# Attention on one core: queries and values computed token by token, mixing matrices in blocks of 64, two batch halves attended together, and the fourth normalisation placed among the attention's instructions

## The reference

```
x = x + conv_gate(_ln_c(x))        # gates; one needs the 0.85 quantile of |x| of each image
t = t + moe(_ln_t(t))              # router, 2 of 8 experts
x = x + attention(_ln_c(x))        # the part that is changed
t = t + ffn(_ln_t(t))              # 8 experts, weights from the mean token

# attention, for each image: q is 8 heads x 16, k and v are 16 wide and shared by all heads
q, k, v = Wq x + bq, Wk x + bk, Wv x + bv
k = softmax(k, over the 256 tokens);  q = softmax(q, over the 16 of a head)
context = k v^T (16 x 16);  out = q context;  y = Wo out + bo
```

## Time and profile before

| | us |
|---|---|
| runs | 245.97, 247.32, 249.61 |
| profiled execution | 246.73 |
| its span in the trace | 244.9 |

### The profile page before, as it was taken

The page is one execution under the profiler, slowest core; times in us unless marked ns, Lnnn a source line. Parts: engine busy times, 40 slices in busy tenths (PEclk is TensorE's granted clock), DMA queues, the critical chain, the costliest instruction groups (busy, mean ns, idle before and its releaser), DMA issues.

```text
span 244.9 us, 3059 instructions
## 1 busy us (share of the span) xinstructions
PE 191.9 (78%) x1077; PEld 78.2 (32%) x1077; DVE 158.1 (65%) x296; ACT 115.8 (47%) x193; POOL 73.9 (30%) x81
## 2 busy tenths in 40 slices
PE   7971478388899689988786788643999999999971
PEld 4310123133261222222222567311346345333220
DVE  1564889674749766687547875998361436647772
ACT  2498677134678765500066924441062695465200
POOL 7710876003699000000350053665340071000000
PEclk9997555559997999999999959997696799999998
DMA  6993100000000000000000000000000000001011
GB/s 185 353 209 76 27 1 0 0 1 0 3 1 3 0 1 3 0 0 0 0 0 3 0 0 3 1 0 1 0 0 3 0 0 0 24 22 46 0 44 43
DMA packets 4291, 6.44 MB, mean 26 GB/s; under 512 B 626, under 2 KB 3954, under 8 KB 4130
## 3 DMA queue, kind: packets, MB, share of 16 engines
q1 hardware_dynamic: 3700, 5.73, 8.6%
q10 hardware_dynamic: 576, 0.52, 0.7%
HBM read 3.99 MB, written 1.05 MB: 21 GB/s over the span
## 4 chain that ended last, share of the span: by engine, by line
PE 47%; DVE 23%; ACT 12%; issue 7%; POOL 6%; DMA 3%; SPq 1%; DVEq 0%
PE ps L742 5%; PE ps L607 4%; PE ps L335 4%; PE ps L753 4%; PE ps L582 4%; PE ps L766 4%; PE ps L329 3%; POOL hidden_of_all_tokens L339 3%; PE ps L555 3%; POOL gated_x L1510 2%; DVE hidden_of_all_tokens L353 2%; PE ps L594 2%; PE ps L570 2%; DVE hidden_of_all_tokens L1288 2%; PE ps L702 2%
## 5 line engine op out<-in xcount | busy, mean ns | idle before, releaser
L339 POOL TENSOR_TENSOR hidden_of_all_tokens<-hidden_of_all_tokens 128x512 f32<-128x512 f32 x16 | 18.5, 1166 | 64.8 <-DVE hidden_of_all_tokens L353 64.8
L1003 ACT ACTIVATE hidden_of_all_tokens<-ps,bn_shift,bn_scale 128x512 f32<-128x512 f32 x32 | 23.2, 776 | 19.9 <-PE ps L742 19.9
L1412 DVE SCALAR_TENSOR_TENSOR gated_x<-ps,bn_shift_negated,hidden_of_all_tokens 128x512 f32<-128x512 f32 x32 | 22.5, 746 | 14.8 <-PE ps L756 13.6
L345 ACT ACTIVATE hidden_of_all_tokens<-ps,weights 128x512 f32<-128x512 f32 x16 | 10.9, 683 | 42.5 <-PE ps L335 40.1
L1288 DVE TENSOR_TENSOR hidden_of_all_tokens<-hidden_of_all_tokens,ps 128x512 f32<-128x512 f32 x32 | 20.5, 683 | 8.7 <-PE ps L594 8.5
L934 ACT ACTIVATE hidden_of_all_tokens<-ps,weights 128x512 f32<-128x512 f32 x32 | 19.9, 685 | 9.5 <-PE ps L582 9.2
L353 DVE COPY hidden_of_all_tokens<-ps 128x512 f32<-128x512 f32 x16 | 11.1, 692 | 19.1 <-PE ps L329 14.0
L742 PE MATMUL ps<-x_normed,weights 64*64 64x512 f32 x128 | 23.2, 656 | 0.2 <-ACT hidden_of_all_tokens L1003 0.2
L335 PE MATMUL ps<-hidden_of_all_tokens,weights 128*128 128x512 f32 x32 | 17.3, 628 | 5.3 <-POOL hidden_of_all_tokens L339 5.1
L582 PE MATMUL ps<-x_normed,weights 64*64 64x512 f32 x128 | 18.4, 667 | 2.1 <-ACT hidden_of_all_tokens L934 2.0
L766 PE MATMUL ps<-gated_x,weights 64*64 64x512 f32 x32 | 16.5, 595 | 2.0 <-DVE x_resid L1420 1.4
(11 more groups left out here) (252 smaller groups left out, 408.0 us busy)
## 6 DMA issues: line engine op xcount, KB each, us to landing
weights<-in_weights SPq DMA_DIRECT2D x1, 2087.5 KB, 12.8
hidden_of_all_tokens<-hidden_of_all_tokens SPq DMA_DIRECT2D x8, 128.0 KB, 4.5
out_x<-x_resid SPq DMA_DIRECT2D x8, 128.0 KB, 2.4
x_resid<-in_x ACTq DMA_DIRECT2D x4, 128.0 KB, 3.2
x_resid<-in_x SPq DMA_DIRECT2D x4, 128.0 KB, 3.6
weights<-in_weights SPq DMA_DIRECT2D x1, 419.0 KB, 6.4
taps_shifted<-taps_padded SPq DMA_DIRECT2D x9, 18.1 KB
weights<-in_weights SPq DMA_DIRECT2D x1, 130.0 KB, 2.4
```

Source lines behind the costliest of these rows:

```text
L339: pool.tensor_tensor(SQ[:, cols(q)], XC[:, cols(q)], XC[:, cols(q)], ALU.mult).then_inc(sq_ready, 1)
L1003: act.activation(h1_tile(t), tile_of(t, Z1_BANK), ACT.Relu, bias=bn_c[:, p:p + 1], scale=bn_a[:, p:p + 1]).then_inc(h1_ready, 1)
L1412: dve.scalar_tensor_tensor(HW[:, t % PAIRS].rearrange("p (b n) -> p b n", n=N), tile_of(t, Z2_BANK).rearrange("p (b n) -> p b n", n=N), ne ...
```

## The change

Queries: T is now the stationary operand in blocks of 64 channels x 128 tokens, `wq` the moving one, so that queries come out with tokens on partitions. The bias is added by a bfloat16 matmul (a stack of three parts, `BQ`, against ones). DVE's two 32x32 turns per step are gone. ACT copies the queries to QB, the softmax is as before, four transposes on TensorE (`queries_back`) bring 128x512 queries back, and ACT stores them to QS (`queries_store`). Tile i is now half h of column group u, i = 2u + h, so `attend` and `attn_add` work on 512 columns and come four times. Keys are made in four row groups of 32 so that the softmax over tokens works on 128 partitions and two tiles; values are made with tokens on partitions by 16 matmuls. BD is made of 64x64 blocks. Normalisation 3 and `f_route` stand among the attention's instructions. SP issues 11 more transfers ahead of L415, with 32 or 128 pieces of 4 bytes each, and 6 more behind L430; POOL has 3 more memsets at its start and 5 small operations before the channel gating.

The cut below leaves out the lines that are removed (they stand above), the shapes of the new tiles, and functions whose body only changed in its tile.

```diff
...
-            return (0, 1, 4, 5)[q] if n == 2 else (0, 1, 5, 6)[q]
+            return ((0, 1, 5, 6), (0, 1, 5, 6), (0, 1, 4, 5), (2, 2, 0, 1))[n][q]
+        def query_bank(i):
+            return i % 2 + (4 if i // HALVES == 1 else 0)
+        def var_bank(n, q):
+            return 3 if n == 3 else 2 + q % 2
         def ln_pe_center(pe, n, q, x_wait):
...
+            a = AT["kv_bias"][0]
+            with nc.allow_non_contiguous_dma(reason="a column of biases"):
+                for j in range(4):
+                    sp.dma_start(kb4[32 * j:32 * j + 32, :], weights_dram[0:32, a:a + 1]).then_inc(kb_in, 16)
+                sp.dma_start(vb[:, :], weights_dram[32:64, a:a + 1]).then_inc(kb_in, 16)
             sp.wait_ge(rows_zeroed, 1)
+            a = AT["bq"][0]
+            with nc.allow_non_contiguous_dma(reason="a column of biases turned into rows"):
+                for h in range(HALVES):
+                    for k in range(PARTS):
+                        sp.dma_start(bq_rows[C * h + k:C * h + k + 1, :], weights_dram[:, a:a + 1].rearrange("p o -> o p")).then_inc(bq_in, 16)
             a, b = AT["sel"][0], AT["b2"][0]
             for h in range(HALVES):
                 for k in range(PARTS):
@@ -428,6 +456,11 @@
                     tap = 3 * dy + dx
                     off = LEAD + (dy - 1) * PITCH + dx - 1
                     sp.dma_start(SHIFTED[tap:18:TAPS, :], PADDED[tap:18:TAPS, off:off + FLAT]).then_inc(shifted_in, 16)
+            sp.wait_ge(bq_split, 4)
+            for h in range(HALVES):
+                for k in range(PARTS):
+                    at_row = slice(C * h + k, C * h + k + 1)
+                    sp.dma_start(BQ[at_row, :], bq_parts[at_row, k]).then_inc(bq_stacked, 16)
...
+            def queries(u):
+                if u == 1:
+                    pe.wait_ge(xc_copied, 3 * NQ)
+                if u >= 2:
+                    pe.wait_ge(q_copied, 4 * u - 6)
+                for h, rows in enumerate((LO, HI)):
+                    pe.matmul(PS[:, query_bank(2 * u + h)].rearrange("p (k c) -> p k c", c=P), ones16[rows, :], BQ[rows, :].unsqueeze(1).to_broadcast([C, 4, P]),
+                              start=True, stop=False, skip_group_check=True)
+                for k in range(4):
+                    for h, rows in enumerate((LO, HI)):
+                        last = pe.matmul(PS[:, query_bank(2 * u + h), cols(k, P)], T[rows, cols(4 * u + k, P)], w("wq", rows, cols(h, P)),
+                                         start=False, stop=True, skip_group_check=True)
+                last.then_inc(q_ready, 1)
+            def queries_back(i):
+                pe.wait_ge(qn_ready, i + 1)
+                pe.wait_ge(*((qs_ready, i - 1) if i >= 2 else (q_copied, 3 + i)))
+                for k in range(4):
+                    last = pe.transpose(PS[:, 4 + i % 2, cols(k, P)], QB[:, i % 4, cols(k, P)], w("ident"))
+                last.then_inc(qt_ready, 1)
+            def attend(u):
+                pe.wait_ge(qs_ready, 2 * u + 2)
+                if u >= 2:
+                    pe.wait_ge(x3_ready, u - 1)
+                for b in range(2):
+                    for h in range(HALVES):
+                        last = pe.matmul(PS[cols(h, C), 6 + u % 2, cols(b, N)], MB[:, h, 2 * u + b], QS[:, (2 * u + h) % 4, cols(b, N)], start=True, stop=True)
+                last.then_inc(a_ready, 1)
...
+                    queries(0)
...
+                for b in (2 * q, 2 * q + 1):
+                    j = b % 4
+                    last = pe.matmul(PS[32 * j:32 * j + 32, 6 + b // 4, 0:N], w("wkv", cols=slice(0, 32)), T[:, cols(b, N)], start=True, stop=True)
+                if q % 2:
+                    last.then_inc(k_ready, 1)
+                if q == 2:
+                    queries(1)
             pe.wait_ge(ln_taken, 3 * NQ)
+            for t in range(16):
+                last = pe.matmul(PS[:, 3, cols(t, 32)], T[:, cols(t, P)], w("wkv", cols=slice(32, 64)), start=True, stop=True)
+            last.then_inc(v_ready, 1)
...
+            def keys_turn(g):
+                pe.wait_ge(ek_ready, g + 1)
+                for jj in range(2):
+                    last = pe.transpose(PS[:, 6 + g, cols(jj, P)], EK[:, cols(2 * g + jj, P)], w("ident"))
+                last.then_inc(kt_ready, 1)
...
+            queries_back(0)
...
+            queries_back(1)
             queries(2)
-            queries(3)
-            for h in range(HALVES):
+            def mixes(h):
                 pe.wait_ge(bd_ready, h + 1)
                 for b in range(BH):
-                    last = pe.matmul(PS[:, 4 + h, cols(b, C)], BD[:, h * BH + b], w("wo"), start=True, stop=True)
+                    for rows in (LO, HI):
+                        last = pe.matmul(PS[rows, 6 + h, cols(b, C)], BD[rows, h * BH + b], w("wo", rows), start=True, stop=True)
...
+            mixes(0)
+            mixes(1)
+            queries_back(2)
+            queries_back(3)
+            queries(3)
+            pe.wait_ge(mb_out, HALVES)
+            attend(0)
+            queries_back(4)
+            center3(0)
+            queries_back(5)
+            attend(1)
+            ln_pe_var(pe, 3, 0)
+            queries_back(6)
+            center3(1)
+            queries_back(7)
+            attend(2)
+            ln_pe_var(pe, 3, 1)
+            attend(3)
+            pe.wait_ge(q_copied, BH)
+            center3(2)
+            f_route(0)
+            center3(3)
+            ln_pe_var(pe, 3, 2)
+            f_route(1)
+            ln_pe_var(pe, 3, 3)
+            f_route(2)
+            f_route(3).then_inc(fl_ready, 1)
...
+            def queries_out(i):
+                act.wait_ge(q_ready, i // HALVES + 1)
+                if i >= 4:
+                    act.wait_ge(qt_ready, i - 3)
+                act.activation(QB[:, i % 4], PS[:, query_bank(i)], ACT.Copy).then_inc(q_copied, 1)
...
+            def queries_store(i):
+                act.wait_ge(qt_ready, i + 1)
+                if i >= 4:
+                    act.wait_ge(a_ready, i // HALVES - 1)
+                act.activation(QS[:, i % 4], PS[:, 4 + i % 2], ACT.Copy).then_inc(qs_ready, 1)
...
             queries_out(0)
+            keys_exp(0)
             queries_out(1)
-            for g in range(2):
-                act.wait_ge(ekt_ready, g + 1)
-                act.activation(EKVT[:, cols(g)], PS[:, 4 + g], ACT.Copy).then_inc(ekt_out, 1)
+            keys_exp(1)
             queries_exp(0)
-            act.wait_ge(cx_ready, 1)
-            act.activation(CTX[:, :], PS[0:32, 2, 0:N], ACT.Copy).then_inc(cx_out, 1)
             queries_out(2)
+            act.wait_ge(v_ready, 1)
+            act.activation(V[:, :], PS[:, 3], ACT.Copy).then_inc(v_out, 1)
+            keys_out(0)
+            keys_out(1)
             queries_exp(1)
             queries_out(3)
...
+            act.activation(CTX[:, :], PS[0:32, 2, 0:N], ACT.Identity, bias=vb[:, 0:1]).then_inc(cx_out, 1)
+            queries_exp(2)
+            queries_store(0)
+            queries_store(1)
+            queries_out(4)
+            queries_exp(3)
+            mixes_out(0)
+            mixes_out(1)
+            queries_store(2)
+            queries_out(5)
+            queries_exp(4)
+            queries_store(3)
+            queries_out(6)
+            queries_exp(5)
+            queries_store(4)
+            queries_out(7)
+            queries_exp(6)
+            queries_store(5)
+            queries_exp(7)
+            ln_act_rstd(act, 3, 0, 1)
+            queries_store(6)
+            queries_store(7)
+            for u in range(1, NQ):
+                ln_act_rstd(act, 3, u, 1)
...
+            keys_max(0)
+            queries_max(0)
+            keys_max(1)
+            keys_scale(0)
+            queries_max(1)
+            keys_scale(1)
...
+            queries_sum(0)
+            queries_max(2)
+            queries_sum(1)
+            queries_max(3)
+            dve.wait_ge(heads_ready, 1)
+            dve.wait_ge(mask4_ready, 1)
...
+            queries_sum(2)
+            queries_max(4)
+            queries_sum(3)
+            queries_max(5)
+            queries_sum(4)
+            queries_max(6)
+            attn_add(0)
+            queries_sum(5)
+            queries_max(7)
+            ln_dve_copy(dve, 3, 0)
+            queries_sum(6)
+            attn_add(1)
+            queries_sum(7)
+            ln_dve_scale(dve, 3, 0, lambda _: dve.wait_ge(q_ready, NQ))
+            ln_dve_copy(dve, 3, 1)
+            attn_add(2)
+            attn_add(3)
+            ln_dve_copy(dve, 3, 2)
+            ln_dve_scale(dve, 3, 1)
+            ln_dve_copy(dve, 3, 3)
+            ln_dve_scale(dve, 3, 2)
+            ln_dve_scale(dve, 3, 3)
...
+            queries_sub(0)
+            for i in range(1, BH):
+                queries_sub(i)
+                queries_norm(i - 1)
+            ln_pool_square(pool, 3, 0)
+            queries_norm(BH - 1)
+            for u in range(1, NQ):
+                ln_pool_square(pool, 3, u)
...```
```

(2 more changed lines are left out.)

304 lines of the change are left out of this document (126 added, 178 removed).

## The result

| | kernel before | changed kernel |
|---|---|---|
| median of the runs | 247.56 us (245.97 to 249.61) | 240.2 us (238.14 to 243.9) |
| ratio | 1 | 0.968, 95% interval 0.959 to 0.977: faster |
| profiled execution, its span | 246.73, 244.9 | 238.14, 236.3 |
| mean granted clock in it | 0.879 | 0.904 |

What follows compares the result with a forecast made beforehand. No engine full: a serial search behind eight transfers, then DVE in the attention loop. Front +2.2, stage -8.1 (-13.1 at full clock, +5.0 for low clock) gave -5.9 from 246.73, 0.6 added for the median: 241.4 us, range 235 to 248.

Steps and rivals of the forecast that it cites:

- The front: Start of the serial search: 11 more transfers in SP's queue delay it by 3.2 - 1.0 = +2.2 us, bounds 0 to +5.7.
- Prices on PE: PE's preparation work at full clock: queries(u) 1.25 us, values 3.7, four transposes 0.64, mixing 1.4 per 32 instructions.
- The preparation: Stage up to the first attended tile: at full clock it comes at 150.7 instead of 152.2, -1.5 us.
- The loop: Attention loop, attend(0) to attend(3): the bound passes from DVE to POOL and ACT, 14.7 us instead of 20.1, -5.4.
- Rival 5: Attention loop not shortened: hand-overs between four engines keep 3.1 us per tile, total 246.8 us; chance 0.05.
- The tail: Normalisation 3 and routing after attend(3): 8.9 us instead of 15.0, routing ends at 174.3, -6.1 us.
- The clock: Two low stretches in the stage, one after values and contexts, one after 155, cost +5.0 us.
- rival 2: PE stays at 2.4 GHz through the stage, having fewer idle gaps: 236.4 us; chance 0.18.
- sum at full clock: Preparation, loop and tail without low clock: -1.5 - 5.4 - 6.1 = -13.1 us.
- rival 6: Slower: clock at 1.2 GHz from 141.5 until the routing, transposes not counting as busy; 254.4 us, chance 0.05.
- The sum: Whole kernel: +2.2 - 8.1 = -5.9 us, profiled execution 240.8, median of the runs 241.4 us.
- rival 3: The front costs its upper bound, +5.7 us, the rest as forecast: 244.9 us; chance 0.10.

Runs made afterwards that it cites:

- experiment 1: Changed kernel with its 11 small bias transfers issued behind the tap transfers, POOL's split of bq moved behind its additions to X: 235.66 us, ratio 0.953.
- experiment 2: Kernel before plus only the 11 bias transfers, their tiles and the memset of bq_rows, read by nobody: 251.74 us, ratio 1.022.
- Experiment 6: Changed kernel with late bias transfers, chunk 6 transposes and attend(3) ahead of the variance products, chunk 6 store ahead of the first rstd: 234.97 us, ratio 0.948.
- Experiment 3: Changed kernel with normalisation 3 behind the attention loop, in the order and banks of the kernel before: 242.96 us, ratio 0.986.
- experiment 9: Changed kernel with late bias transfers, 14 extra unread matmuls in PE's gaps and the other order of woven steps: 233.31 us, ratio 0.945.
- experiment 10: Changed kernel with late bias transfers and 14 extra unread matmuls, plus 28 more in the search at the front: 237.1 us, ratio 0.964.
- experiment 7: Changed kernel with whole mixing matrices, 16 products of 128 rows instead of 32 of 64: 241.93 us, ratio 0.977.
- experiment 4: Kernel before with 21 extra unread matmuls where PE idles between the keys and the end of the attention loop: 244.55 us, ratio 0.989.

## Why the prediction was right, and where it was wrong

**The front, forecast +2.2: this term was mis-sized.** The mechanism was right, SP's queue; the size is 4.5 us on the mean of the profiles, 4.5 and 4.2 by the medians of experiments 1 and 2, and 3.8 and 5.5 by their ratios. Two steps failed. The 11 issues were counted at 5.3 us and took 6.8: the key columns, taken at the price of 8-piece transfers, cost 0.42 to 1.08 each (the 1.08 goes with the place in the queue, as the last section tells), so SP reached the search's transfers at 18.4 and not at 16.6. And the landing, lowered from 4.5 to 3.5, went up instead. In all five profiles with the new transfers ahead the eight are issued back to back and the last of them, for which the search waits, lands after 5.4 to 5.6 us; in the seven without them SP waits for data in between and the last lands after 3.6 to 4.7. Nothing came back. The value lies inside the bounds (0 to 5.7); the choice within them was a hope that the row for output transfers would apply, when the nearer row was that of the same transfers. The remaining 1.5 us or so of the 6.0 in the two profiles isn't the change's: the search of the kernel before started 1.1 us ahead of the mean of its kind, with the earliest normalisation 0 of all, and that of the change 0.4 behind.

**Prices on PE: mostly right.** `queries(u)` 1.25 forecast, 1.2 measured (134.73 to 135.94). By the Trainium skill, TensorE: Matmul & The Clock Gate, section on LDWEIGHTS, a load's time follows its columns and not its rows. Here the trace agrees, other than the prediction says: a load of L689, 64 rows by 128 columns, lasts 188 ns, and one of 128 rows by 128 columns in the kernel before (L722) 186 to 192. The prediction's 2.2 us took the loads of the two halves one after the other; in the trace they start in pairs, 4 ns apart or less, one pair every 111 ns. The row of pairs, 0.058 us per load, was the right one to go by. Values 3.7 and 3.76, four transposes 0.64 and 0.66. Mixing was taken at 2.8 for both halves and cost 2.08. The preparation gained 3.0 us instead of 1.5: mixing gave 0.7 of the difference, and the two first `queries` with the keys, which took 4.0 us (134.7 to 138.7) instead of 4.6, most of the rest.

**The loop, forecast 14.7: 14.7.** Rival 5, a loop that isn't shortened, is out. DVE's work per tile fell as forecast and PE's waits went to POOL, the squares above all. Experiment 6 shows what the 14.7 hold: 2.8 us of them are the order, the variance products that stand ahead of the transposes of chunk 6 and of `attend(3)`.

**The tail, forecast 8.9: 9.6.** Experiment 3 gives the worth of the weaving: 4.0 us of tail against 1.5 us of loop.

**The clock, forecast +5.0: this term failed.** No low stretch lay in the stage in either profile of the change, bar 1.9 us at its end in the second; this was rival 2's course. Together the three parts and the clock made -13.9, where the sum at full clock had said -13.1. What a low stretch costs came out at the lower end of the 2 to 3 us per 6.8 that were forecast: experiments 6 and 9 have the same order of steps, one with some 12 us at the low clock and 57.9 us of stage, the other, with the extra matmuls, with none and 54.0, so 2.2 us per 6.8. In the kernel before, where DVE carries the loop, it was less: 13.7 us at the low clock for 2.9.

Where the clock can fall was foreseen better than how often. The forecast had one stretch behind values and contexts and one behind 155. In the nine profiles with the change's attention the first came four times and the second once, never both. In experiments 6 and 10 the clock fell at 136.5 and 140.2, each time within 0.3 us after the last product of the values; in experiments 1 and 7 it fell at 139.4 and 141.8, during them; in experiment 3 it fell at 160.7, in the loop; in the four others, with the same products, nowhere before 178. **What decides it stays open.** The extra matmuls don't settle it: they were in experiment 10 as well. Nor do small instructions alone: the window of 148.0 to 151.4 holds 78 of them, transposes among them, and the granted clock is 1.00 in it and behind it. With that rival 6 loses its ground. By the Trainium skill, TensorE: Matmul & The Clock Gate, part on the PE-mode transpose, transposes don't count as busy; no run here shows them bringing the clock down.

**The sum.** 240.2 against 241.4 looks like an accurate forecast. It was +6.0 in the traces (+4.5 of it the change's) instead of +2.2 for the front, -13.9 instead of -8.1 for the stage since the clock penalty of 5.0 was missing, -0.7 instead of nothing for the last block, and a median 2.1 above the profiled execution instead of 0.6; these make the -1.2. The near hit is luck: two errors of 3.8 and 5.8 us cancelled for the most part. Had the two low stretches come at their forecast price, 240.2 + 5.0 = 245.2 us would be the estimate, close to rival 3.

## What to carry to other kernels

Before small transfers are put into a queue, look at what the same queue issues next and who waits for it: 11 transfers of at most 512 bytes, needed 100 us later, cost 4.5 us because they stood ahead of eight that a serial search waited for, and behind them they cost nothing that shows. Where an order is written by hand, weaving the next stage in took 4.0 us off the tail for 1.5 us of loop; standing it behind the instructions that the loop's end waits for, not ahead of them, was worth another 1.2 us in one pair of traces, too little for the times to show. And compare stages at the same granted clock, for instance with unread matmuls in the gaps, before the difference is laid to the work.

## What was not expected of the hardware

- The same kind of issue has several prices on SP. Four key columns took 2.53 us at 6.7, while the weights came in, with the DMA engines busy throughout, and 1.80 at 31.3 in experiment 1, with a DMA share of 0.09. The 1.08 us of the first goes with its place: in experiments 1 and 10 the first of `share_rows`, with 8 pieces, stands there (6.3) and takes 1.15 and 1.39. `f_wo`, ahead of all that changed, cost 1.19 for two before and 1.65 after.
- In normalisation 0 the centring products took 0.59 us each in the median in the kernel before and 1.06 in the changed one, and the column of the granted clock shows 1.00 in both. But the trace's record of the clock begins only at 4.7 us in the one and at 10.0 in the other, and the column shows 1.00 where there is no record. At a recorded 1.2 GHz the same product takes 1.06 us too (L329 behind 173), and 0.59 at 2.4. So the clock came up late. These are the rows of the first six of these instructions in the two kernels:

```profile
4.71 2.94 PE L329 MATMUL ps<-x_resid,weights 128*128 128x512 f32 x6 [0.33 <-DMA x_resid<-in_x]
```

```profile
4.98 5.30 PE L347 MATMUL ps<-x_resid,weights 128*128 128x512 f32 x6 [0.60 <-DMA x_resid<-in_x]
```

- Over the twelve profiles the record of the clock begins at 4.7 to 10.8 us and the sum over `x_normed` starts at 16.3 to 18.9, nearly in the same order, and the search follows it where nothing else is late. The change doesn't bring it: the second profile of the change has 4.7, and experiment 4, whose front is the old one, 8.8. What brings the clock up late wasn't tried; PE starts at 1.5 us in all of them.
- The clock fell at 136.5 in experiment 6 behind 18.2 us of which PE was busy for 16, and it stayed up in the change behind 3.4 us of which PE was busy for 2.3 (175.6 to 179.0).
- 28 extra matmuls in the search kept 2.4 GHz only until 31, and the way from the search to the end of the experts took 2.4 us longer with them than without.
